# Attention stage: value products of four key pairs in one run, and the denominators of an octet as one round of 512 and one of 256 columns

## The chip, the cores and the metric

The program runs on one core of one Trainium2 chip. The number that counts is the device time of one execution in microseconds. The kernel before took 5224.2 us, the median of three runs (5220.57, 5224.20 and 5231.23).

## What is computed

Two layers follow one another on an image of 512 channels and 64 x 64 pixels (4096 tokens), in float32. The change is in the first one's attention: 16 heads of 32 channels, each a full softmax over 4096 x 4096 scores.

```python
q_in = x
qn = group_norm(x, gn_w, gn_b)
vn = group_norm(qn, gn_w, gn_b)
q, k, v = to_tokens(conv1x1(qn, wq, bq)), to_tokens(conv1x1(vn, wk, bk)), to_tokens(conv1x1(vn, wv, bv))
attn = jax.nn.softmax(jnp.einsum('bhnd,bhmd->bhnm', q, k) * scale, axis=-1)
out = jnp.einsum('bhnm,bhmd->bhnd', attn, v)
out = conv1x1(out.transpose(0, 1, 3, 2).reshape(B, C, H, W), wo, bo)
return (out + q_in) / jnp.sqrt(jnp.float32(2.0))
```

The second layer (a projection, a 5x5 depthwise convolution, linear attention, a projection with batch norm) is not touched.

## The kernel before

The program has five stages in a row, with all engines meeting between them: `stage_qkv`, `stage_attention`, `stage_output`, `stage_linear`, `stage_project`. Only `stage_attention` changes, and it is the longest one.

**Units, pairs, octets.** The stage works through 64 units, 4 per head, of 1024 queries each. A unit goes over 32 key tiles of 128 keys. Two key tiles are a pair (16 per unit), and four pairs are an octet (4 per unit). Eight units (two heads) are a turn; the first and the last turn are written out, and the six between them are a hardware loop.

**The products of TensorE.** For each key tile there are two score products (L642) into one of three PSUM banks `pscore`, 512 queries each. In between go the maximum products (L629): the scores of a unit that is one or two ahead, whose row maxima are needed before its exponentials can be shifted. There are four of them per pair, as many as there are score products, so the two kinds alternate. They go into a ring of four PSUM banks `pmax`. Both kinds are float32r with a stationary operand of 128 columns.

**Value products** (`times_v`, L655) multiply the exponentials of a pair with the values. A pair takes four matmuls of 512 columns (two key tiles by two halves of the queries); each has a stationary operand of 32 columns and writes its own 32 partitions of the bank `pout`, so the four stand side by side in the array. They are plain float32, which TensorE's records show as two instructions each: 8 matmul records for a pair, which are two passes of four side by side. They are issued in runs of `RUN` pairs, at the end of every `RUN`-th pair's scores, for pairs that lie `RUN` to 2 x `RUN` - 1 pairs back.

**Denominators** (`denominators`, L660 to L671) are column sums over the keys. GpSimd adds exponentials beforehand (`eight_steps`, L598 to L611): of the eight tiles in an octet it adds tiles 0, 1, 2 into one sum and 3, 4, 5 into another, and tiles 6 and 7 stay as they are (`RAW` = 6). TensorE then multiplies with a column of ones: four matmuls on the two sums, four on the two raw tiles, 512 columns each, again two records each, so four passes of four. They come once per octet, behind the run of value products of every fourth pair, and go into a bank of the `pmax` ring, which ScalarE copies out (`read_den`, L747).

**What the other engines do.** ScalarE turns each score bank into exponentials (L781), two per key tile, into `prob`, which holds 16 tiles. It also copies `pout` out once per unit (`read_out`, L741) at key tile `OUT_AT` = 2 x `RUN`, the denominators once per octet, and the next head's values once per head (`copy_v`, L756) at key tile 12 of the head's second unit. VectorE takes the row maxima of each `pmax` bank (L808). Once per unit, at pair 14, it reduces them further (`top`, L814); TensorE turns the result (`transpose_shift`, L636) in a bank of the same ring, ScalarE and VectorE split the turned numbers into a high and a low part (L753, L820), and SyncE sends them into the query operand of the next unit. So in that one place a maximum product has only three others between itself and the one whose bank it takes over.

**The order is written out.** Each engine's instructions are issued in program order. A maximum product waits until VectorE has read the bank it takes over, four places back in the ring (`bank_free`). A score product waits for the exponential of the score three back. In `turn` (L685) the order within a pair is: score, maximum, score, maximum, score, maximum, score, then a run of value products and the denominators if they are due, then the fourth maximum.

Of the kernel before, what the change touches and what calls it, by code (L numbers as in the profile page):

```python
# [11 lines left out]
ALU = mybir.AluOpType  # L12
# [8 lines left out]
BANK = 512  # L21
# [5 lines left out]
HD = C // HEADS  # L27
# [7 lines left out]
def done(n):  # L35
    return n + CREDIT
# [306 lines left out]
def stage_attention(nc, x, scr, v_tok, x1, x_in, ident_d):  # L343
# [11 lines left out]
    HS = 2 * KT  # L355
    OCT = 8
    OCTS = KT // OCT
    ADDS = 4
    RAW = 6
    SUMS = 3 * HD  # L360
    FULL = SUMS + 2
    QT = UNIT // P
# [12 lines left out]
    AHEAD = MAXES + EARLY * PER_PAIR  # L375
    T_AT = PER_PAIR

    RUN = 2
    OUT_AT = 2 * RUN
    with ExitStack() as ctx:  # L380
        def sb(name, shape, dt=F32):
            return ctx.enter_context(nc.sbuf_tensor(name, shape, dt))

        def pb(name, shape):
            return ctx.enter_context(nc.psum_tensor(name, shape, F32))

        def sem(name):
            return ctx.enter_context(nc.semaphore(name))
# [4 lines left out]
        prob = sb("b_prob", [P, PBUF, UNIT])  # L393
        sums = sb("b_sums", [P, 2, 2, UNIT])
        ones = sb("b_ones", [P, 1])
# [8 lines left out]
        pmax = [pb(f"b_pmax{i}", [P, BANK]) for i in range(RING)]  # L404
# [8 lines left out]
        exped = sem("b_exped")  # L413
        times_v_done = sem("b_times_v_done")
        pool_added = sem("b_pool_added")
# [180 lines left out]
        @block.gpsimd  # L596
        def _(pool):
            def eight_steps(g, b):  # L598

                p = prob[:, b * OCT:(b + 1) * OCT, :]  # L600


                pool.wait_ge(den_done, done(g - 1))
                for s in range(2):
                    at = 3 * s
                    pool.wait_ge(exped, done((g * OCT + at + 2) * 2))
                    pool.tensor_tensor(sums[:, b, s, :], p[:, at, :], p[:, at + 1, :], ALU.add).then_inc(pool_added, 1)  # L607
                    pool.wait_ge(pool_added, done(g * ADDS + 2 * s + 1))
                    pool.wait_ge(exped, done((g * OCT + at + 3) * 2))
                    pool.tensor_tensor(sums[:, b, s, :], sums[:, b, s, :], p[:, at + 2, :],  # L610
                                       ALU.add).then_inc(pool_added, 1)  # L611

            with pool.Fori(0, ALL * OCTS // 2) as j:
                for b in range(2):
                    eight_steps(j * 2 + b, b)
# [7 lines left out]
        def _(pe):  # L623
# [21 lines left out]
            def times_v(u, head, par, c, pair):  # L645
                if pair == 0:
                    pe.wait_ge(out_read, done(u))
                    if c == 0:
                        pe.wait_ge(v_in, done(head + 1))
                pe.wait_ge(exped, done(u * HS + (2 * pair + 2) * 2))  # L650
                for half in range(2):
                    for odd in range(2):
                        kt = 2 * pair + odd
                        row = (half * 2 + odd) * HD
                        mm = pe.matmul(pout[row:row + HD, :], vst[:, par, kt, :],  # L655
                                       prob[:, kt % PBUF, half * BANK:(half + 1) * BANK],
                                       start=(pair == 0), stop=(pair == PAIRS - 1))
                mm.then_inc(times_v_done, 1)

            def denominators(bank, u, o):  # L660
                pe.wait_ge(pool_added, done((u * OCTS + o + 1) * ADDS))
                pe.wait_ge(exped, done((u * OCTS + o + 1) * OCT * 2))
                for raw in range(2):
                    for half in range(2):
                        for s in range(2):
                            row = (half * 2 + s) * HD
                            terms = prob[:, o % 2 * OCT + RAW + s, :] if raw else sums[:, o % 2, s, :]
                            mm = pe.matmul(pmax[bank][row:row + 1, :], ones[:],  # L668
                                           terms[:, half * BANK:(half + 1) * BANK],
                                           start=(raw == 0), stop=(raw == 1))  # L670
                mm.then_inc(den_done, 1)  # L671

            pe.wait_ge(q_in[0], done(48))
# [11 lines left out]
            def turn(i, first, final):  # L685
                for u, head, par, c in units(i):
# [3 lines left out]
                    for pair in range(PAIRS):  # L690
# [11 lines left out]
                        def one_maximum(n):  # L702
                            if products:
                                bank_free(pe, u, "max", PER_PAIR * pair + n)
                                max_product(bank_of(c, "max", PER_PAIR * pair + n), products[n], t_par, t_buf)

                        for part in range(4):
                            scores(u, 4 * pair + part, par, place % QBUF)
                            if part < 3:
                                one_maximum(part)  # L710
                        if pair % RUN == RUN - 1:
                            for old in range(pair - 2 * RUN + 1, pair - RUN + 1):
                                if old >= 0:
# [3 lines left out]
                        if pair % (OCT // 2) == OCT // 2 - 1:  # L717
                            o = pair // (OCT // 2)
                            if o or behind:
                                bank_free(pe, u, "den", o)  # L720
                                denominators(bank_of(c, "den", o), u if o else u - 1, (o - 1) % OCTS)
# [8 lines left out]
            turn(TURNS - 1, False, True)  # L730
            for pair in range(PAIRS - RUN, PAIRS):
                times_v(ALL - 1, HEADS - 1, 1, UNITS - 1, pair)
            bank_free(pe, ALL, "den", 0)
            denominators(bank_of(0, "den", 0), ALL - 1, OCTS - 1)

        @block.scalar
        def _(act):
# [21 lines left out]
            def unit(u, head, par, c, behind, values, shift):  # L759
                for kt in range(KT):  # L760
# [3 lines left out]
                    if kt % OCT == 0:  # L764

                        act.wait_ge(pool_added, done((u * OCTS + kt // OCT - 1) * ADDS))

# [885 lines left out]
def conv_seq(nc, x, chan, wqT, wkT, wvT, bv, bo, woT, w_all, dw_all, pw_all, wprojT, chan_bn,  # L1653
             group_mean, mask, hmask, ident, out):
    scr = Scratch(nc)
    with nc.sbuf_tensor("v_tok", [P, N // P, C], F32) as v_tok, nc.semaphore("x_in") as x_in:

        x1 = v_tok[:].rearrange("p (k a) c -> p k (a c)", k=KC)
        stage_qkv(nc, x, chan, wqT, wkT, wvT, bv, group_mean, scr, v_tok)
        stage_attention(nc, x, scr, v_tok, x1, x_in, ident)  # L1660
        stage_output(nc, x1, x_in, bo, woT, ident, scr)
        stage_linear(nc, w_all, dw_all, pw_all, mask, hmask, ident, scr, x1)
        stage_project(nc, wprojT, chan_bn, scr, x1, out)
# [49 lines left out]
```

## Time and profile before

| | |
|---|---|
| three runs, median | 5224.2 us |
| the profiled execution | 5231.3 us |
| its span in the trace | 5229.4 us |
| TensorE matmuls busy over the span | 4989.3 us (95%) |
| VectorE busy | 3575.3 us (68%) |
| ScalarE busy | 2878.2 us (55%) |
| GpSimd busy | 2477.0 us (47%) |
| attention stage, from its first maximum product to its last product | 335.6 to about 3858 us |

Busy times are sums over the whole program. Matmul records overlap, so their durations add up to more than the time that passes; the distance between the starts of two neighbours is what one costs. The middle of the attention stage repeats with a fixed period per octet, so one octet read closely stands for some 250.

### The profile page before, as it was taken

The numbers are of one execution on the slowest core, as the hardware profiler recorded it, in microseconds if no ns is written. First come the engines' busy times: TensorE is split into PE (matmuls) and PEld (weight loads), VectorE is DVE, ScalarE is ACT, GpSimd is POOL, SyncE is SP. The second block draws the span as 40 slices with busy tenths as digits, with TensorE's granted clock in tenths as the row PEclk, the third lists the DMA queues.
The fourth block names the chain that finished last, engine by engine and source line by source line (L and its number), as shares of the span: only waits on it lengthen the run. The fifth ranks groups of instructions, "written<-read, shape, count | busy, mean of one in ns | idle before, by whom it ended". The sixth has DMA issues, their size and how long they took to land. (4 is left out here: it accounts for less than half of the span.)

```text
span 5229.4 us, 103029 instructions
## 1 busy us (share of the span) xinstructions
PE 4989.3 (95%) x34768; PEld 2766.3 (53%) x34768; DVE 3575.3 (68%) x4898; ACT 2878.2 (55%) x5445; POOL 2477.0 (47%) x1068
## 2 busy tenths in 40 slices
PE   7989999999999999999999999999978999999697
PEld 6855555555555555555555555555536655555343
DVE  4357777776777777777777777777725887889523
ACT  2216666666666666666666666666651445544402
POOL 0007676776766667667677676677630000000000
PEclk9979999999999999999999999999989999999898
DMA  4330000000000000000000000001031000000254
GB/s 155 129 101 12 24 17 24 24 17 25 17 24 16 26 24 17 25 24 17 25 17 24 25 17 24 17 24 65 22 110 55 12 32 23 31 26 22 80 156 139
DMA packets 101917, 217.38 MB, mean 42 GB/s; under 512 B 13616, under 2 KB 22960, under 8 KB 98864
## 3 DMA queue, kind: packets, MB, share of 16 engines
q1 hardware_dynamic: 101424, 210.81, 12.9%
q8 instruction: 309, 5.06, 0.4%
q14 instruction: 184, 1.51, 0.1%
HBM read 130.54 MB, written 79.69 MB: 40 GB/s over the span
## 5 line engine op out<-in xcount | busy, mean ns | idle before, releaser
L808 DVE TENSOR_REDUCE b_mx<-b_pmax 128x1 f32<-128x512 f32 x4096 | 2507.3, 683 | 935.7 <-PE b_pmax L629 932.9
L781 ACT ACTIVATE b_prob<-b_pscore 128x512 f32<-128x512 f32 x4096 | 2089.8, 619 | 350.1 <-PE b_pscore L642 345.0
L607 POOL TENSOR_TENSOR b_sums<-b_prob 128x1024 f32<-128x1024 f32 x512 | 1220.7, 2384 | 1332.5 <-ACT b_prob L781 1332.5
L629 PE MATMUL b_pmax<-b_kst,b_qst 96*128 96x512 f32 x4096 | 1716.0, 422 | 17.9 <-DMA b_qst<-scratch_ql 15.2
L642 PE MATMUL b_pscore<-b_qst,b_kst 98*128 98x512 f32 x4096 | 1633.7, 400 | 13.8 <-issue 5.0
L610 POOL TENSOR_TENSOR b_sums<-b_sums,b_prob 128x1024 f32<-128x1024 f32 x512 | 1220.5, 2384 | 89.7 <-POOL b_sums L607 86.7
L629 PEld LDWEIGHTS b_pmax<-b_kst,b_qst 96*128 96x128 f32 x4096 | 784.8, 192 | 672.3 <-DVE b_mx L808 287.9
L655 PE MATMUL b_pout<-b_prob,b_vst 128*32 128x512 f32 x8192 | 992.1, 602 | 0.0
L642 PEld LDWEIGHTS b_pscore<-b_qst,b_kst 98*128 98x128 f32 x4096 | 781.0, 191 | 194.2 <-ACT b_prob L781 29.3
L1486 DVE SCALAR_TENSOR_TENSOR d_dsum<-d_ypad,d_dw,d_dsum 128x2048 f32<-128x2048 f32 x288 | 680.9, 2364 | 10.2
L747 ACT ACTIVATE b_outd<-b_pmax 128x512 f32<-128x512 f32 x256 | 153.2, 599 | 765.6 <-PE b_pmax L668 765.6
L655 PEld LDWEIGHTS b_pout<-b_prob,b_vst 128*32 128x32 f32 x8192 | 214.6, 109 | 485.3 <-ACT b_prob L781 282.6
L1397 ACT ACTIVATE d_piece_x<-d_pdw 32x512 f32<-32x512 f32 x384 | 226.3, 589 | 327.0 <-PE d_pdw L1295 313.9
L1250 POOL TENSOR_TENSOR d_num_w<-d_vks,d_mask 128x128 f32<-128x128 f32 x8 | 8.7, 1084 | 799.4 <-ACT d_vks L1438 799.4
L1279 PE MATMUL d_pmain<-v_tok,d_w 128*128 128x512 f32 x768 | 350.7, 600 | 17.7 <-DVE d_tv_x L1462 11.0
L1295 PE MATMUL d_pdw<-d_ypad,d_wtap 32*32 32x512 f32 x9600 | 319.1, 610 | 26.7 <-ACT d_piece_x L1397 25.8
L1295 PEld LDWEIGHTS d_pdw<-d_ypad,d_wtap 32*32 32x32 f32 x9600 | 222.1, 103 | 118.0 <-issue 45.9
L668 PE MATMUL b_pmax<-b_sums,b_ones 128*1 128x512 f32 x2048 | 266.6, 592 | 0.0
L668 PE MATMUL b_pmax<-b_prob,b_ones 128*1 128x512 f32 x2048 | 266.5, 592 | 0.0
L1577 PE MATMUL f_ps<-f_num,f_w 128*128 128x512 f32 x512 | 222.0, 597 | 34.4 <-DVE f_num L1616 34.4
L1279 PEld LDWEIGHTS d_pmain<-v_tok,d_w 128*128 128x128 f32 x768 | 140.7, 191 | 182.1 <-issue 172.3
L1577 PEld LDWEIGHTS f_ps<-f_num,f_w 128*128 128x128 f32 x512 | 98.0, 192 | 159.3 <-issue 159.3
(159 smaller groups left out, 2251.8 us busy)
## 6 DMA issues: line engine op xcount, KB each, us to landing
b_kst<-scratch_kh SPq DMA_DIRECT2D x32, 512.0 KB, 10.5
b_qst<-scratch_qh SPq DMA_DIRECT2D x128, 128.0 KB, 2.9
scratch_att<-b_outn SPq DMA_DIRECT2D x128, 128.0 KB
scratch_num<-d_num SPq DMA_DIRECT2D x64, 256.0 KB, 2.0
f_num<-scratch_num SPq DMA_DIRECT2D x8, 2048.0 KB, 9.7
f_rden<-scratch_rden SPq DMA_DIRECT2D x64, 256.0 KB, 9.7
v_tok<-in_x SPq DMA_DIRECT2D x8, 1024.0 KB, 12.8
scratch_qh<-a_high SPq DMA_DIRECT2D x8, 1024.0 KB, 4.2
```

Of the source, the lines that this page charges most:

```text
L607: pool.tensor_tensor(sums[:, b, s, :], p[:, at, :], p[:, at + 1, :], ALU.add).then_inc(pool_added, 1)
L610: pool.tensor_tensor(sums[:, b, s, :], sums[:, b, s, :], p[:, at + 2, :], ALU.add).then_inc(pool_added, 1)
L629: pe.matmul(pmax[bank][:], qst[0:SUMS, b, t * P:(t + 1) * P], kst[0:SUMS, par, j * BANK:(j + 1) * BANK], start=True, stop=True).then_inc(m ...
L642: pe.matmul(pscore[score_bank(hs)][:], kst[0:FULL, par, kt * P:(kt + 1) * P], qst[0:FULL, b, at], start=True, stop=True).then_inc(scored, 1)
L655: mm = pe.matmul(pout[row:row + HD, :], vst[:, par, kt, :], prob[:, kt % PBUF, half * BANK:(half + 1) * BANK], start=(pair == 0), stop=(pa ...
L668: mm = pe.matmul(pmax[bank][row:row + 1, :], ones[:], terms[:, half * BANK:(half + 1) * BANK], start=(raw == 0), stop=(raw == 1))
L781: act.activation(prob[:, kt % PBUF, half * BANK:(half + 1) * BANK], pscore[score_bank(hs)][:], ACT.Exp, scale=SCALE).then_inc(exped, 1)
L808: dve.tensor_reduce(mx[:, b, t, j:j + 1], pmax[bank][:], AX.X, ALU.max).then_inc(max_read, 1)
L1279: mm = pe.matmul(pmain[:], w[:, b, k, :], x1[:, k, n * BANK:(n + 1) * BANK], start=(k == 0), stop=(k == KC - 1))
L1295: mm = pe.matmul(pdw[r][c * BLK:(c + 1) * BLK, :].rearrange("p (r c) -> p r c", c=IMG), wtap[rows, b, tap, :], ypad[rows, b, y:y + ROWS, d ...
L1486: add = dve.scalar_tensor_tensor(acc, src, dw[:, b, tap:tap + 1], acc, ALU.mult, ALU.add)
L1577: mm = pe.matmul(ps[b * KC + t][:], w[:, m, t * P:(t + 1) * P], num[:, b, m, :], start=(m == 0), stop=(m == MS - 1))
```

## The change

`RUN` goes from 2 to 4: the value products of four pairs stand in one run, at every fourth pair, in front of that octet's denominators. `OUT_AT`, which hangs on it, goes from key tile 4 to key tile 8. `RAW` goes from 6 to 7: GpSimd adds tiles 0 to 3 into one sum and 4 to 6 into the other, five additions instead of four. The one raw tile left is split in columns: of each half of 512 queries, the first 256 columns are added to the rows of the first sum and the other 256 to the rows of the second. So the second round of denominators has four matmuls of 256 columns.

```diff
-    ADDS = 4
-    RAW = 6
+    ADDS = 5
+
+    RAW = 7
...
-    RUN = 2
+    RUN = 4
     OUT_AT = 2 * RUN
...
                 pool.wait_ge(den_done, done(g - 1))
-                for s in range(2):
-                    at = 3 * s
-                    pool.wait_ge(exped, done((g * OCT + at + 2) * 2))
-                    pool.tensor_tensor(sums[:, b, s, :], p[:, at, :], p[:, at + 1, :], ALU.add).then_inc(pool_added, 1)
-                    pool.wait_ge(pool_added, done(g * ADDS + 2 * s + 1))
-                    pool.wait_ge(exped, done((g * OCT + at + 3) * 2))
-                    pool.tensor_tensor(sums[:, b, s, :], sums[:, b, s, :], p[:, at + 2, :],
-                                       ALU.add).then_inc(pool_added, 1)
+                for s, tiles, before in ((0, (0, 1, 2, 3), 0), (1, (4, 5, 6), 3)):
+                    acc = sums[:, b, s, :]
+                    pool.wait_ge(exped, done((g * OCT + tiles[1] + 1) * 2))
+                    pool.tensor_tensor(acc, p[:, tiles[0], :], p[:, tiles[1], :], ALU.add).then_inc(pool_added, 1)
+                    for n, tile in enumerate(tiles[2:]):
+                        pool.wait_ge(pool_added, done(g * ADDS + before + n + 1))
+                        pool.wait_ge(exped, done((g * OCT + tile + 1) * 2))
+                        pool.tensor_tensor(acc, acc, p[:, tile, :], ALU.add).then_inc(pool_added, 1)
...
-                for raw in range(2):
-                    for half in range(2):
-                        for s in range(2):
-                            row = (half * 2 + s) * HD
-                            terms = prob[:, o % 2 * OCT + RAW + s, :] if raw else sums[:, o % 2, s, :]
-                            mm = pe.matmul(pmax[bank][row:row + 1, :], ones[:],
-                                           terms[:, half * BANK:(half + 1) * BANK],
-                                           start=(raw == 0), stop=(raw == 1))
+                for half in range(2):
+                    for s in range(2):
+                        row = (half * 2 + s) * HD
+                        pe.matmul(pmax[bank][row:row + 1, :], ones[:],
+                                  sums[:, o % 2, s, half * BANK:(half + 1) * BANK], start=True, stop=False)
+
+                for half in range(2):
+                    for s in range(2):
+                        row, at = (half * 2 + s) * HD, s * (BANK // 2)
+                        mm = pe.matmul(pmax[bank][row:row + 1, at:at + BANK // 2], ones[:],
+                                       prob[:, o % 2 * OCT + RAW, half * BANK + at:half * BANK + at + BANK // 2],
+                                       start=False, stop=True)
                 mm.then_inc(den_done, 1)
```

TensorE's order at the end of an octet's scores, in the first turn. `b_pmax` are maximum products (and the denominators' bank), `b_pscore` score products, `b_pout` value products. Before:

```order
L629 MATMUL b_pmax3<-b_kst,b_qst 128x512
L642 MATMUL b_pscore1<-b_qst,b_kst 128x512
L629 MATMUL b_pmax0<-b_kst,b_qst 128x512
L642 MATMUL b_pscore2<-b_qst,b_kst 128x512
L655 MATMUL b_pout<-b_prob,b_vst 32x512 x8
L668 MATMUL b_pmax1<-b_sums,b_ones 1x512 x4
L668 MATMUL b_pmax1<-b_prob,b_ones 1x512 x4
L629 MATMUL b_pmax2<-b_kst,b_qst 128x512
```

The same place of the kernel with the change:

```order
L629 MATMUL b_pmax3<-b_kst,b_qst 128x512
L642 MATMUL b_pscore1<-b_qst,b_kst 128x512
L629 MATMUL b_pmax0<-b_kst,b_qst 128x512
L642 MATMUL b_pscore2<-b_qst,b_kst 128x512
L655 MATMUL b_pout<-b_prob,b_vst 32x512 x16
L666 MATMUL b_pmax1<-b_sums,b_ones 1x512 x4
L672 MATMUL b_pmax1<-b_prob,b_ones 1x256 x4
L629 MATMUL b_pmax2<-b_kst,b_qst 128x512
```

Before, eight value products stand here and eight more in the middle of the octet, 8 maximum and 8 score products away on either side. Now all sixteen stand here, and from one such place to the next 16 maximum and 16 score products follow each other with nothing in between.

ScalarE's order around the copy of the value products, before (key tile 4 of a unit). `b_outn` is that copy, `b_outd` the copy of the denominators, `b_prob` the exponentials:

```order
L781 ACTIVATE b_prob<-b_pscore0 128x512 [waits b_scored]
L781 ACTIVATE b_prob<-b_pscore1 128x512 [waits b_scored]
L741 ACTIVATE b_outn<-b_pout 128x512 [waits b_out_stored,b_times_v_done]
L781 ACTIVATE b_prob<-b_pscore2 128x512 [waits b_scored]
L781 ACTIVATE b_prob<-b_pscore0 128x512 [waits b_scored]
```

With the change (key tile 8):

```order
L785 ACTIVATE b_prob<-b_pscore2 128x512 [waits b_scored]
L785 ACTIVATE b_prob<-b_pscore0 128x512 [waits b_scored]
L751 ACTIVATE b_outd<-b_pmax2 128x512 [waits b_den_done,b_den_stored,b_pool_added,b_times_v_done]
L745 ACTIVATE b_outn<-b_pout 128x512 [waits b_out_stored,b_times_v_done]
L785 ACTIVATE b_prob<-b_pscore1 128x512 [waits b_scored]
```

The copy of the value products, which stood alone at key tile 4, now stands right behind that of the denominators at key tile 8.

## Rows read from the trace of the kernel before

**Rows 1.** The page: engines' busy time, TensorE's clock in 40 slices, one group's mean ns.

```profile
PE 4989.3 (95%) x34768; PEld 2766.3 (53%) x34768; DVE 3575.3 (68%) x4898; ACT 2878.2 (55%) x5445; POOL 2477.0 (47%) x1068
...
PEclk9979999999999999999999999999989999999898
...
L668 PE MATMUL b_pmax<-b_sums,b_ones 128*1 128x512 f32 x2048 | 266.6, 592 | 0.0
```

**Rows 2.** Windows, the attention stage's middle: stretch, busy by engine, clock, DMA.

```profile
410.00:3790.00 3380.00, 3368.92 (x19993) 1780.71 (x19995) 2456.70 (x4112) 2222.09 (x4377) 2366.60 (x997) 1.00 0.08 23
```

**Rows 3.** Timeline, TensorE, one octet: start, duration, engine, line, operation.

```profile
1205.82 0.50 PE L629 MATMUL b_pmax<-b_kst,b_qst 96*128 96x512 f32 x1
1206.16 0.39 PE L642 MATMUL b_pscore<-b_qst,b_kst 98*128 98x512 f32 x1
1206.40 0.39 PE L629 MATMUL b_pmax<-b_kst,b_qst 96*128 96x512 f32 x1
...
1209.44 0.39 PE L642 MATMUL b_pscore<-b_qst,b_kst 98*128 98x512 f32 x1
1209.76 1.92 PE L655 MATMUL b_pout<-b_prob,b_vst 128*32 128x512 f32 x16
1211.61 0.50 PE L629 MATMUL b_pmax<-b_kst,b_qst 96*128 96x512 f32 x1
...
1215.55 1.92 PE L655 MATMUL b_pout<-b_prob,b_vst 128*32 128x512 f32 x16
1217.29 1.04 PE L668 MATMUL b_pmax<-b_sums,b_ones 128*1 128x512 f32 x8
1218.15 1.04 PE L668 MATMUL b_pmax<-b_prob,b_ones 128*1 128x512 f32 x8
1219.12 0.50 PE L629 MATMUL b_pmax<-b_kst,b_qst 96*128 96x512 f32 x1
```

**Rows 4.** Timeline, VectorE: the same burst's reads, and the stage's first 64.

```profile
1206.36 4.88 DVE L808 TENSOR_REDUCE b_mx<-b_pmax 128x1 f32<-128x512 f32 x8 [2.63 <-PE b_pmax L629]
...
336.36 38.36 DVE L808 TENSOR_REDUCE b_mx<-b_pmax 128x1 f32<-128x512 f32 x64 [6.25 <-PE b_pmax L629]
```

**Rows 5.** Timeline, the burst with the transposition, three engines.

```profile
1238.21 0.19 PEld L629 LDWEIGHTS b_pmax<-b_kst,b_qst 96*128 96x128 f32 x1 [0.84 <-DVE b_mx L808]
...
1238.75 0.69 DVE L808 TENSOR_REDUCE b_mx<-b_pmax 128x1 f32<-128x512 f32 x1 [0.91 <-PE b_pmax L629]
...
1239.62 3.07 DVE L808 TENSOR_REDUCE b_mx<-b_pmax 128x1 f32<-128x512 f32 x5
...
1240.95 0.19 PEld L629 LDWEIGHTS b_pmax<-b_kst,b_qst 96*128 96x128 f32 x1 [0.23 <-DVE b_mx L808]
...
1241.55 0.19 PEld L629 LDWEIGHTS b_pmax<-b_kst,b_qst 96*128 96x128 f32 x1 [0.30 <-DVE b_mx L808]
...
1242.14 0.19 PEld L629 LDWEIGHTS b_pmax<-b_kst,b_qst 96*128 96x128 f32 x1 [0.30 <-DVE b_mx L808]
...
1242.48 0.39 PE L642 MATMUL b_pscore<-b_qst,b_kst 98*128 98x512 f32 x1
...
1242.80 1.92 PE L655 MATMUL b_pout<-b_prob,b_vst 128*32 128x512 f32 x16
```

**Rows 6.** Timeline, ScalarE, an octet in which the values are copied.

```profile
1098.18 0.60 ACT L747 ACTIVATE b_outd<-b_pmax 128x512 f32<-128x512 f32 x1 [3.23 <-PE b_pmax L668]
1098.67 4.02 ACT L781 ACTIVATE b_prob<-b_pscore 128x512 f32<-128x512 f32 x8
1102.49 1.14 ACT L756 ACTIVATE b_vst<-v_tok 128x1024 f32 x1
1104.34 0.60 ACT L781 ACTIVATE b_prob<-b_pscore 128x512 f32<-128x512 f32 x1 [0.71 <-PE b_pscore L642]
```

**Rows 7.** Timeline, GpSimd, the first two of an octet's four additions.

```profile
1208.74 2.38 POOL L607 TENSOR_TENSOR b_sums<-b_prob 128x1024 f32<-128x1024 f32 x1 [3.44 <-ACT b_prob L781]
1211.29 2.40 POOL L610 TENSOR_TENSOR b_sums<-b_sums,b_prob 128x1024 f32<-128x1024 f32 x1 [0.17 <-POOL b_sums L607]
```

## The prediction, made before the changed kernel ran

> **What bounds the kernel now.** I read the page's engine table first. TensorE is busy 95% of the span, VectorE 68%, and the clock row shows nine tenths or more nearly everywhere [rows 1]. The window over the middle of the attention stage is sharper: of 3380 us TensorE's matmuls fill 3368.9, at a granted clock of 1.00, which is 2.4 GHz [rows 2]. So the stage goes at TensorE's pace, and what matters is what an octet costs there. The timeline gives it to the hundredth: the first maximum product of one octet starts at 1205.82 us and that of the next at 1219.12, so an octet takes 13.30 us [rows 3].
>
> Its parts, all from rows 3. A burst of 8 maximum and 8 score products lasts 3.94 (1205.82 to 1209.76). From the second maximum product at 1206.40 to the last score at 1209.44 there are 13 steps in 3.04, 0.234 each, so a maximum and a score together cost 0.467. A run of value products for two pairs lasts 1.85 in front of a burst (1209.76 to 1211.61) and 1.74 in front of the denominators (1215.55 to 1217.29). The denominators' first two passes take 0.86, so a pass of four matmuls side by side costs 0.43; the last two take 0.97 up to the next maximum product, 0.11 more. The value products' first pass costs 1.74 - 3 x 0.43 = 0.45.
>
> Each change from bursts to runs and back costs 1.85 - 1.74 = 0.11 on leaving a run, 0.34 - 0.23 = 0.11 at the first score after it, 0.32 - 0.23 = 0.09 on entering (1209.44 to 1209.76), and 0.02 in the first pass: 0.33 us. There are two changes per octet.
>
> **Without any wait the change saves 0.76 us per octet.** One of the two changes goes: -0.33. One 512-column round of two passes (0.86) becomes a 256-column round. Nothing in the trace has this shape. Its upper bound is the full pass, 0.43, from the nearest row; the lower one is half of it, 0.215, since a pass's time is that of its columns and the four matmuls of a pass start close together: eight records of 0.592 [rows 1] fill 1.04 us [rows 3], and 1.04 - 0.43 - 0.59 leaves 0.02 for the spread of four starts. I take 0.215, so the round saves 0.43. A price below half would need columns to go faster than they do in any row. Fewer instructions elsewhere are nothing, as they pass beside the array's work.
>
> The Trainium skill has a rule that speaks against half: in "TensorE: Matmul & The Clock Gate" (Part 1) a matmul decoded by the sequencer's own code costs about 62 ns, which bounds small matmuls. Four of them would be an estimated 0.25 us per pass, and the sum would come out 18 us higher; four starts within 0.02 us in the rows speak against it.
>
> **What the long burst adds: VectorE cannot follow it.** VectorE reads 64 banks in 38.36 us, back to back: (38.36 - 0.68) / 63 = 0.598 us from one to the next, with 0.68 for the read itself; the burst's 8 reads give the same (4.88 - 0.68) / 7 = 0.60 [rows 4]. TensorE makes a bank every 0.467 [rows 3]. In a burst of 8 the ring of four banks and the run behind it absorb the difference. In a burst of 16 they don't.
>
> Count from the start of the burst's first maximum product, number 0. VectorE starts reading it 0.54 later (1205.82 to 1206.36), so read k starts at 0.54 + 0.598 k and ends 0.68 later. Maximum product k takes over the bank of k - 4, and its weight load starts about 0.05 after that read's end: in rows 5 the reads that begin at 1239.62 + 0.598 and + 2 x 0.598 end 0.68 later, at 1240.90 and 1241.50, and the loads start at 1240.95 and 1241.55. This gives 0.60 k - 1.12 as the earliest start of load k. Without waiting it starts at 0.35 + 0.467 (k - 1). They cross between k = 7 and k = 8. So before, bursts of 8 (k up to 7) just never waited; with the change every maximum product from the ninth on waits. The last, k = 15, loads at 0.54 + 0.598 x 11 + 0.68 + 0.05 = 7.85. From such a delayed load the score behind it follows 0.34 later and the run 0.32 after that (1242.14, 1242.48, 1242.80, [rows 5]). The burst lasts 7.85 + 0.66 = 8.51, where 16 unhindered ones would take 3.94 + 8 x 0.467 = 7.68. That is 0.83 us of waiting per octet.
>
> The trace of before already contains this wait at full clock, which is why I trust it. In the burst with the transposition the look-back is one shorter, and three maximum loads in a row stand 0.60 apart, each with idle time in front that ends on VectorE's read [rows 5].
>
> The new octet is then 8.51 (burst) + 0.45 + 7 x 0.43 (values, 3.46) + 2 x 0.43 + 2 x 0.215 + 0.11 (denominators, 1.40) = 13.37 us, against 13.30: **+0.07 us**. Over some 250 octets (64 units of 4, less those at the end that have no maximum products) this is +18 us.
>
> **The octet with the transposition.** There VectorE's reduction `top` stands between two reads and pushes the later ones by 0.26: the reads at 1238.75 and 1239.62 are 0.87 apart in place of 0.60 [rows 5]. In the middle of a long burst this delay is no longer absorbed, and the last maximum product looks back three reads, not four: it loads at 0.54 + 0.598 x 12 + 0.26 + 0.68 + 0.05 = 8.71, so the burst lasts 9.37, or 0.86 over the normal one. Before, the same burst lasted 4.59 (1238.21 to 1242.80) against 3.94, 0.65 over. This adds 0.21 in each of 62 units: +13 us. What hangs on the transposition (the split numbers and their transfer into the next unit's queries) has the longer run to hide in, 4.9 us in place of 3.6; nothing there.
>
> **ScalarE.** Exponentials follow each other every (4.02 - 0.60) / 7 = 0.49 us at most [rows 6], slower than scores come unhindered (0.467) but faster than VectorE's 0.598, so ScalarE is the second limit and hidden by the first. The copy of `pout` moves behind that of the denominators and delays the exponentials by 0.5 in one octet of four. Scores then come at 0.49 from the fourth on, 0.25 late, and VectorE's pace has overtaken that by the fifteenth: I take nothing; the bound above is 0.25 in each of 64, 16 us. The value copy (1.14 us) at key tile 12 stood behind a run and was mostly covered by it: it runs from 1102.49 to 1103.63, and the next exponential waits 0.71 for its score [rows 6]. With the change no run stands there. The first exponential comes 1.2 after the burst's start (two copies of 0.5 behind the denominators' end), the ninth 8 x 0.49 and the value copy of 1.0 later, at 6.1; its bank is free at 6.7, and the scores from the twelfth on follow ScalarE at 0.49: the last one at about 8.8 where VectorE alone allows 8.2. That is +0.6 for 15 heads: +9 us.
>
> **GpSimd** gets a fifth addition. It starts its first 2.92 after the octet's start (1208.74) and needs 5 x 2.39 plus three waits on itself of 0.17 [rows 7], 12.46 us, to 15.4. The next octet's first addition comes at 13.37 + 2.92 = 16.3. It keeps up with 0.9 to spare, and the denominators ask for the sums only at the end of the next octet, 9 us later. Nothing.
>
> **Queues.** SyncE's store of `outn` waits for key tile 8 in place of 4, and behind it are the loads of queries three units ahead and of the next head's keys. They are needed more than one unit (53 us) later. Nothing. At the two ends of the stage and at the loop's returns the order shifts by a run; I take nothing, between -5 and +5 us.
>
> **The sum.** 18 + 13 + 9 = +40 us on the profiled execution's 5231.3 (its span of 5229.4 and 1.9 around it), so 5271; that execution is 7.1 over the median of the three runs, so against the median 5224.2 + 40 = **5264 us**. It is a small difference of large terms: -190 us saved (0.76 x 250), +208 us waited (0.83 x 250), and 22 more.
>
> **Rivals.**
>
> *VectorE's pace does not bind.* The place is the wait of maximum products 8 to 15. If bank or read behaved better in a long burst than rows 5 show, TensorE would keep 12.5 us per octet, and GpSimd's 12.46 and ScalarE's 16 x 0.49 would sit just under it: 250 x -0.76 = -190, +9 for the copy, 5043 us. It turns faster from the point at which the wait is under 0.6 us per octet. For it speaks only the average: VectorE is busy 2457 of 3380 us [rows 2]. Against it, the three waiting loads. 0.06.
>
> *The wait is 0.1 us shorter than worked out,* as each term is a reading to a hundredth and the ring starts with some slack. Then all cancels: 5224 to 5234, no difference. 0.10.
>
> *The 256-column round costs more than half.* At the full 0.43 per pass, 2 x 0.215 x 250 = +108: 5372. That it saves nothing gets 0.04; something between (0.25 to 0.3, 5280 to 5305) 0.10.
>
> *ScalarE's two copies in a row are not overtaken.* +16: 5280. 0.06. "TensorEngine Tiling (Array Packing)" in the Trainium skill (Performance Considerations) warns that tiling speeds TensorE and not the emptying of PSUM; that is this rival and my forecast in one, and the rows price it.
>
> The forecast itself has 0.64, with its own range of 5244 to 5285.
>
> **Numbers.** A measurement of this kernel can tell about 0.2%, 10 us, from no change. Below 5214: 0.06. Within: 0.10, mostly the second rival. Above 5234: the rest, 0.84. The range for 8 in 10 goes from 5236 to 5300: it leaves out the two sub-cases on the fast side and the full-price round.
>
> **What the changed profile would show.** Octets of 13.3 to 13.45 us on TensorE's timeline. Reads of VectorE in groups of 16 over 9.65 us (15 x 0.598 + 0.68). Weight loads of the later maximum products 0.60 apart, with idle time that ends on `b_mx`. Idle before them of some 200 us in total that was not there. TensorE's busy share in the middle falls below 99.7%. The last denominators' round 0.43 + 0.11 long. If instead the maximum products stay 0.467 apart to the end of the burst, the forecast is wrong and the kernel is 190 us faster; if the burst is 8.5 and the octet is not 13.4, the 256-column round was mispriced.

## The result, and the profile after

The changed kernel takes 5373.2 us (median of three runs, 5365.4 to 5373.6) against 5224.2 us: a ratio of 1.0278, 95% interval 1.0255 to 1.0302. It is slower, as forecast, but by 149 us where 40 were forecast, and outside the range that ended at 5300. The profiled execution spans 5371.3 us, 141.9 more than before.

First what came as worked out. TensorE's timeline of one octet (start, duration, engine, line, operation), which answers to [rows 3]:

```profile
1236.42 0.50 PE L629 MATMUL b_pmax<-b_kst,b_qst 96*128 96x512 f32 x1
...
1243.08 0.50 PE L629 MATMUL b_pmax<-b_kst,b_qst 96*128 96x512 f32 x1
...
1243.68 0.50 PE L629 MATMUL b_pmax<-b_kst,b_qst 96*128 96x512 f32 x1
...
1244.28 0.50 PE L629 MATMUL b_pmax<-b_kst,b_qst 96*128 96x512 f32 x1
1244.61 0.40 PE L642 MATMUL b_pscore<-b_qst,b_kst 98*128 98x512 f32 x1
1244.94 3.64 PE L655 MATMUL b_pout<-b_prob,b_vst 128*32 128x512 f32 x32
1248.40 1.04 PE L666 MATMUL b_pmax<-b_sums,b_ones 128*1 128x512 f32 x8
1249.26 0.61 PE L672 MATMUL b_pmax<-b_prob,b_ones 128*1 128x256 f32 x8
1249.80 0.50 PE L629 MATMUL b_pmax<-b_kst,b_qst 96*128 96x512 f32 x1
```

The burst takes 8.52 us (1236.42 to 1244.94; forecast 8.51), the value products 3.46 (3.46), the denominators 1.40 (1.40), the octet 13.38 (13.37). The last three maximum products stand 0.60 apart. VectorE's reads and one of the weight loads, answering to [rows 4, 5], show why:

```profile
1236.95 9.66 DVE L812 TENSOR_REDUCE b_mx<-b_pmax 128x1 f32<-128x512 f32 x16 [3.73 <-PE b_pmax L629]
...
1244.28 0.19 PEld L629 LDWEIGHTS b_pmax<-b_kst,b_qst 96*128 96x128 f32 x1 [0.30 <-DVE b_mx L812]
```

Sixteen reads without a gap take 9.66 us, and the load was idle 0.30 us until one of them ended. So a steady octet costs 0.08 us more than before. That cannot make 142 us.

The answer is in the list of who waited for whom (total us, times, longest), in lines for which the trace of before has no counterpart:

```profile
ACT b_outd L751 <- DMA scratch_att_den<-b_outd: 161.0, 18, 9.7
...
PEld b_pmax L629 <- ACT b_outd L751: 75.6, 18, 4.9
PE b_pmax L629 <- ACT b_outd L751: 67.9, 18, 4.5
```

Eighteen times ScalarE's copy of the denominators waited for the store of the previous ones, and TensorE for ScalarE. The timeline of one such place, with ScalarE's instructions and SyncE's transfers (SPq; the duration of such a row spans the issues it groups, and `x4` here is this store's two transfers and, at 1313.06, the next store's two):

```profile
1293.63 0.60 ACT L751 ACTIVATE b_outd<-b_pmax 128x512 f32<-128x512 f32 x1 [4.39 <-PE b_pmax L672]
1294.12 0.59 ACT L745 ACTIVATE b_outn<-b_pout 128x512 f32<-128x512 f32 x1
...
1294.90 1.29 SPq L542 DMA_DIRECT2D scratch_att<-b_outn  x2
1296.48 0.89 SPq L527 DMA_DIRECT2D b_qst<-scratch_qh  x2
1297.47 0.73 SPq L527 DMA_DIRECT2D b_qst<-scratch_ql  x1
1298.40 0.56 SPq L523 DMA_DIRECT2D b_kst<-scratch_kh  x1
1299.05 0.37 SPq L523 DMA_DIRECT2D b_kst<-scratch_kl  x1
1299.52 0.37 SPq L523 DMA_DIRECT2D b_kst<-scratch_kh  x1
1300.14 14.16 SPq L549 DMA_DIRECT2D scratch_att_den<-b_outd  x4
...
1312.27 0.60 ACT L751 ACTIVATE b_outd<-b_pmax 128x512 f32<-128x512 f32 x1 [9.65 <-DMA scratch_att_den<-b_outd]
```

`outd` is one buffer. It is filled at 1293.63; SyncE first stores `outn`, loads queries, and once per head loads the next head's keys (three transfers of 512 KB); the store of `outd` follows at 1300.14. The next copy into `outd` is due at about 1307.3 and starts at 1312.27. The packets of the trace show what the store stood behind: its four rows of 2048 bytes move from 1310.68 to 1311.36, two by two right behind the last two 16 KB packets of the keys, which end at 1310.68 and 1311.03. By the semaphore it has landed at 1312.25, 12.1 us after its issue, and the copy starts.

In the kernel before, `outn` was ready at key tile 4, so the keys were issued half an octet earlier. The store followed its copy by 0.8 us in place of 6.5, and had 12.5 us, not 7, until the next copy (SyncE's and ScalarE's timeline of before):

```profile
1262.20 0.32 SPq L522 DMA_DIRECT2D b_kst<-scratch_kh  x1
...
1264.63 0.60 ACT L747 ACTIVATE b_outd<-b_pmax 128x512 f32<-128x512 f32 x1 [2.94 <-PE b_pmax L668]
...
1265.40 14.56 SPq L548 DMA_DIRECT2D scratch_att_den<-b_outd  x4
...
1277.92 0.60 ACT L747 ACTIVATE b_outd<-b_pmax 128x512 f32<-128x512 f32 x1 [2.93 <-PE b_pmax L668]
```

It stood behind the same keys there and landed at 1275.37, 10.0 us after its issue: 2.5 us before it was needed. So the bytes in front of the store were no harm by themselves; the change took away the room for them.

What it costs TensorE (timeline, then windows with busy time by engine and the granted clock before the last two numbers):

```profile
1308.06 0.39 PE L642 MATMUL b_pscore<-b_qst,b_kst 98*128 98x512 f32 x1
...
1312.92 0.56 PE L629 MATMUL b_pmax<-b_kst,b_qst 96*128 96x512 f32 x1 [4.47 <-ACT b_outd L751]
```

```profile
1308.06:1312.92 4.86, 0.39 (x2) 0.00 (x0) 1.14 (x2) 0.65 (x2) 1.07 (x1) 1.00 0.07 15
1313.00:1320.00 7.00, 7.00 (x17) 5.24 (x18) 5.05 (x8) 5.42 (x10) 4.74 (x3) 0.52 0.01 2
1320.00:1322.40 2.40, 2.40 (x11) 1.73 (x9) 2.40 (x5) 2.19 (x5) 2.40 (x2) 0.99 0.00 0
```

TensorE stands still for 4.5 us, and in the 7 us after it the granted clock is 0.52, the lower level of 1.2 GHz. The burst lasts 15.67 us (1306.78 to 1322.44), 7.1 more than normal. There are 14 such bursts, one per head, 5.8 to 7.3 us too long, 93 us together. In the last turn, where SyncE loads the image at the same place, three more bursts are 3.2, 4.8 and 3.2 too long. That is 104 us of the 142; the first experiment shows that the other 38 are the forecast's own 40.

### The profile page after: what moved, and what is told of

Its sections match the earlier page's. It is cut to its first block and busy times, and to the rows that moved or that the text cites. A ratio compares the mean times of both kernels' runs of the same rounds, so it can differ in the third digit from the quotient of the medians.

```text
span 5371.3 us, 103836 instructions
## 1 busy us (share of the span) xinstructions
PE 5024.1 (94%) x34768; PEld 2708.0 (50%) x34768; DVE 3564.0 (66%) x4898; ACT 2928.4 (55%) x5445; POOL 3079.8 (57%) x1324
## 5 line engine op out<-in xcount | busy, mean ns | idle before, releaser
L785 ACT ACTIVATE b_prob<-b_pscore 128x512 f32<-128x512 f32 x4096 | 2141.6, 637 | 47.7 <-PE b_pscore L642 40.5
L629 PE MATMUL b_pmax<-b_kst,b_qst 96*128 96x512 f32 x4096 | 1831.6, 450 | 87.0 <-ACT b_outd L751 67.9
L611 POOL TENSOR_TENSOR b_sums<-b_sums,b_prob 128x1024 f32<-128x1024 f32 x768 | 1826.6, 2378 | 134.2 <-POOL b_sums L607 85.2
L642 PE MATMUL b_pscore<-b_qst,b_kst 98*128 98x512 f32 x4096 | 1687.8, 414 | 23.4 <-ACT b_prob L785 14.0
L629 PEld LDWEIGHTS b_pmax<-b_kst,b_qst 96*128 96x128 f32 x4096 | 797.4, 195 | 705.5 <-DVE b_mx L812 404.1
L655 PE MATMUL b_pout<-b_prob,b_vst 128*32 128x512 f32 x8192 | 940.4, 600 | 0.0
L642 PEld LDWEIGHTS b_pscore<-b_qst,b_kst 98*128 98x128 f32 x4096 | 796.5, 195 | 265.7 <-ACT b_prob L785 164.5
L655 PEld LDWEIGHTS b_pout<-b_prob,b_vst 128*32 128x32 f32 x8192 | 241.3, 110 | 551.8 <-issue 465.4
L672 PE MATMUL b_pmax<-b_prob,b_ones 128*1 128x256 f32 x2048 | 157.3, 379 | 0.0
## 6 DMA issues: line engine op xcount, KB each, us to landing
b_kst<-scratch_kh SPq DMA_DIRECT2D x32, 512.0 KB, 10.8
```

Source lines behind the costliest of these rows:

```text
L611: pool.tensor_tensor(acc, acc, p[:, tile, :], ALU.add).then_inc(pool_added, 1)
L629: pe.matmul(pmax[bank][:], qst[0:SUMS, b, t * P:(t + 1) * P], kst[0:SUMS, par, j * BANK:(j + 1) * BANK], start=True, stop=True).then_inc(m ...
L642: pe.matmul(pscore[score_bank(hs)][:], kst[0:FULL, par, kt * P:(kt + 1) * P], qst[0:FULL, b, at], start=True, stop=True).then_inc(scored, 1)
L655: mm = pe.matmul(pout[row:row + HD, :], vst[:, par, kt, :], prob[:, kt % PBUF, half * BANK:(half + 1) * BANK], start=(pair == 0), stop=(pa ...
L785: act.activation(prob[:, kt % PBUF, half * BANK:(half + 1) * BANK], pscore[score_bank(hs)][:], ACT.Exp, scale=SCALE).then_inc(exped, 1)
```

## The experiments

Each was timed beside the kernel before on the same chip: 5226.2 us for *the denominators' store first*, *VectorE's pace* and *the two halves*, 5224.5 for *the loads first*, *bytes or moment* and *the version that beats both*.

**The denominators' store first.** The changed kernel, SyncE's part of `turn`:

```diff
                         store_den(*old, OCTS - 2)
                         store(*old)
+                        store_den(*old, OCTS - 1)
...
-                    if not (first and place == 0):
-                        store_den(*old, OCTS - 1)
```

> The changed kernel, with one edit on SyncE: the store of the last octet's denominators is issued right behind the store of the value products, ahead of the loads of queries and keys. Theory A: the 109 us beyond the forecast come from ScalarE waiting for that store, whose transfers stand behind 1.5 MB of keys, once per head. Then the rare bursts of 15 us become normal ones of 8.5 us and the time is 5264 us (5254 to 5275), with octets of 13.38 us as before. Rival B: the long bursts come from something else in the long run (GpSimd's fifth addition, the clock), and the store only happens to be late: the time stays at 5373 us and the idle time moves to another releaser.

Measured: 5268.0 us, ratio 1.0076 (1.0059 to 1.0093). Theory A holds, and B falls: the long run, GpSimd's fifth addition and the rest are all still there. The span is 103.3 us shorter than the changed kernel's, against 104 counted in bursts. SyncE's timeline of it:

```profile
1273.72 1.28 SPq L542 DMA_DIRECT2D scratch_att<-b_outn  x2
1275.26 1.60 SPq L549 DMA_DIRECT2D scratch_att_den<-b_outd  x2
1277.16 1.09 SPq L527 DMA_DIRECT2D b_qst<-scratch_qh  x2
...
1279.12 0.32 SPq L523 DMA_DIRECT2D b_kst<-scratch_kh  x1
```

**The loads first.** The other way out: `store(*old)` moves behind the loads, so that these no longer wait for key tile 8.

```diff
                         store_den(*old, OCTS - 2)
-                        store(*old)
...
                     if not (first and place == 0):
+                        store(*old)
                         store_den(*old, OCTS - 1)
```

> The changed kernel, with the other way out on SyncE: the loads of queries and keys are issued at the unit's start, ahead of the store of the value products, which waits for key tile 8. The keys then have 13 us before the denominators' store is issued behind them. Theory A (that store must not stand behind keys in flight): no burst of 15 us, 5264 us (5258 to 5275), the same as with the store ahead of the loads. Rival: if the number of transfers in the unit's first half as such is the trouble, part of the stalls stays, 5300 us or more.

Measured: 5267.2 us, 1.0087 (1.0070 to 1.0103). Theory A holds. The same transfers, with the same bytes, cost nothing where the store isn't behind keys in flight.

**Bytes or moment.** Key loads of an eighth of the size, in the changed kernel's order:

```diff
-                        load_k(head + 1, 1 - par)
+                        for row, name in ((0, "kh"), (HD, "kl"), (2 * HD, "kh")):
+                            sp.dma_start(kst[row:row + HD, 1 - par, 0:BANK].bitcast(F32),
+                                         heads[name][head + 1, :, 0:BANK]).then_inc(k_in[1 - par], 16)
```

> The changed kernel with SyncE's order as it is, but each of the later heads' key loads brings 512 of the 4096 key positions (the rest keeps older keys, so the attention is that of mixed heads). It tells the bytes in front of the store from the moment at which the store is issued. Theory A1 (the store's transfers stand behind the keys' bytes): it lands in 2 to 3 us and the 15 us bursts are gone: 5264 us. Theory A2 (SyncE issues the store too late, after seven other transfers): the issue stays at 6 us after ScalarE's copy, and part of the stall stays, 5300 us or more.

This kernel leaves out seven eighths of each later head's keys, so its output is not the attention's; only its time is used. Measured: 5276.3 us, one run. Its timeline:

```profile
1272.27 0.60 ACT L753 ACTIVATE b_outd<-b_pmax 128x512 f32<-128x512 f32 x1 [4.39 <-PE b_pmax L674]
...
1278.94 21.37 SPq L549 DMA_DIRECT2D scratch_att_den<-b_outd  x5
...
1285.64 0.60 ACT L753 ACTIVATE b_outd<-b_pmax 128x512 f32<-128x512 f32 x1 [4.38 <-PE b_pmax L674]
```

The store is issued 6.7 us after the copy, as late as in the changed kernel (6.5), and the next copy still comes on time. No burst of 15 us is left. The store has landed at 1284.35, 5.4 us after its issue (A1 had 2 to 3), where it took 12.1 in the changed kernel. So A2 falls, as the late issue alone does not stall anything, and A1 holds in that the keys' bytes fill the time. Together with the kernel before, where the same bytes cost nothing behind an earlier issue, it takes both. From the copy to the landing of its store it is 6.5 + 12.1 = 18.6 us in the changed kernel, more than the 13.4 of an octet; it was 0.8 + 10.0 = 10.8 before, and is 6.7 + 5.4 = 12.1 here. What remains over the 5267 of the kernel with the loads first are the image loads of the last turn, which this kernel does not shorten: its list of waits has `ACT b_outd <- DMA` 4 times, 27 us, and the bursts there are 9 us too long in all.

**VectorE's pace.** The first kernel of this section, with the maxima over half the columns:

```diff
-                dve.tensor_reduce(mx[:, b, t, j:j + 1], pmax[bank][:], AX.X, ALU.max).then_inc(max_read, 1)
+                dve.tensor_reduce(mx[:, b, t, j:j + 1], pmax[bank][:, 0:BANK // 2], AX.X, ALU.max).then_inc(max_read, 1)
```

> The first kernel of this set, with VectorE's maxima taken over 256 of the 512 columns of a bank: the maxima leave out half of the keys, so the shift is another; all else stands. Theory A (VectorE's 0.598 us per read sets the long burst): a read takes some 0.38 us, the waits of maximum products 8 to 15 go, ScalarE's 0.48 to 0.49 us per exponential is the next limit: bursts of 7.7 to 7.9 us, octets of 12.55 to 12.75 us, about 5050 to 5090 us. Rival: if TensorE's own order or ScalarE sets the long burst, it stays at 8.5 us and the time at 5264 us.

Its maxima leave out half of the keys. Measured: 5055.4 us, one run. Sixteen reads now keep up with TensorE, and the burst is 7.73 us long (timeline):

```profile
1240.66 0.50 PE L628 MATMUL b_pmax<-b_kst,b_qst 96*128 96x512 f32 x1
...
1248.39 3.64 PE L654 MATMUL b_pout<-b_prob,b_vst 128*32 128x512 f32 x32
...
1241.20 7.47 DVE L811 TENSOR_REDUCE b_mx<-b_pmax 128x1 f32<-128x256 f32 x16 [5.57 <-PE b_pmax L628]
```

Nothing else was touched, so VectorE's read sets the long burst: 8.52 less 7.73 is 0.79 us per octet, and 5268 less 5055 over some 250 octets is 0.85. At this pace ScalarE's copy of the denominators waits for GpSimd (`ACT b_outd <- POOL b_sums`, 686 us, where the first kernel of this section has 6). GpSimd's 12.46 us are then close to the octet's 12.59 (7.73 + 3.46 + 1.40), so GpSimd is probably the next limit; no run tests that.

**The two halves of the change.** The new denominators with `RUN = 2`:

```diff
-    RUN = 4
+    RUN = 2
```

> The changed kernel with RUN back at 2: only the denominators' part of the change (fifth addition on GpSimd, one round of 512 and one of 256 columns). Theory A: a maximum product never waits in bursts of 8, the round saves 2 x 0.215 us per octet, GpSimd's 12.46 us fit into an octet of 12.87 us, and the key loads are issued at key tile 4 as before the change: 5224 - 0.43 x 256 = 5114 us. Rival C: GpSimd or the ring's last bit of slack takes it back (burst 7 crosses its limit by 0.07 us only): octets of 13.0 to 13.3 us, 5150 to 5224 us.

Measured: 5122.6 us, 0.9800 (0.9783 to 0.9816). Bursts of 8 are 3.94 us as before, the denominators 1.40, the octet 12.87; Theory A holds to 0.2%. GpSimd's five additions of 12.46 us fit in with 0.4 to spare (timeline; the first and the last row are the first additions of two octets, 12.87 us apart, and each waits 0.46 or 0.47 us for ScalarE, and not the other way round):

```profile
1196.27 2.38 POOL L607 TENSOR_TENSOR b_sums<-b_prob 128x1024 f32<-128x1024 f32 x1 [0.47 <-ACT b_prob L785]
...
1206.29 2.39 POOL L611 TENSOR_TENSOR b_sums<-b_sums,b_prob 128x1024 f32<-128x1024 f32 x1 [0.17 <-POOL b_sums L607]
1209.14 2.38 POOL L607 TENSOR_TENSOR b_sums<-b_prob 128x1024 f32<-128x1024 f32 x1 [0.46 <-ACT b_prob L785]
```

And `RUN = 4` with the old denominators, SyncE's store ahead of the loads:

```diff
-    RUN = 2
+    RUN = 4
```

> The kernel before with RUN = 4 only (denominators of two full rounds), and with the denominators' store ahead of the loads so that keys are not in its way. Theory A: per octet -0.33 us for one change of kind less, +0.83 us of waiting for VectorE, so 13.80 us, and 22 us for the transposition and the value copy: 5224 + 125 + 22 = 5371 us. Rival: if the waiting for VectorE is only the shadow of the shorter period, it shrinks where the octet is longer, and the time is 5290 us or less.

Measured: 5379.0 us, 1.0291 (1.0274 to 1.0309). Burst 8.52, values 3.46, denominators 1.83: 13.81 us. Theory A holds, 8 us over its figure, and the rival falls: the burst is as long in an octet of 13.81 us as in one of 13.38, so the wait builds up within the burst.

**A version that beats both.** `RUN = 2`, the new denominators, the loads first:

> A candidate for the fastest: RUN = 2 with the new denominators, and the loads issued at the unit's start. Theory A: in octets of 12.87 us nothing waits for a store (in the run without this edit one burst in 64 is 0.12 us long), so the edit brings nothing: 5114 to 5124 us, the same as without it within 0.2%. Rival: if transfers still delay something that is spread thin, it is 10 us or more faster.

Measured: 5120.2 us, 0.9800 (0.9784 to 0.9816), the same as without the last edit. These two, level within the noise, are the fastest versions here that leave nothing out; what makes them so is the denominators' half of the change.

## Why the prediction was right and wrong, point by point

- *The round of 256 columns costs half.* Right: 0.54 us with the way out (1249.26 to 1249.80), 2 x 0.215 + 0.11, and the records of its two passes start 0.216 apart. The bound that the prediction quoted from the Trainium skill ("TensorE: Matmul & The Clock Gate", Part 1), with the prediction's estimate of 0.25 us per pass, did not show. The half-price round alone is worth 104 us (5122.6 against 5226.2; forecast 110).
- *One change between kinds saves 0.33.* Right: values 3.46 and denominators 1.40 to the hundredth, and with two full rounds 13.81, which is 13.30 + 0.83 of waiting - 0.33.
- *VectorE cannot follow.* Right in mechanism and size: 8.52 for 8.51, and the half reads show it is the cause. One sign was off: the idle time of weight loads that ends on `b_mx` grew by 148 us (287.9 before, 436.2 with the denominators' store first), not by some 200.
- *The transposition's burst.* Forecast 9.37; in the trace 9.38 in most units (1263.20 to 1272.58).
- *The value copy at key tile 12, +0.6.* Right: those bursts last 9.10 us. ScalarE's timeline has the 1.16 us copy at 906.92, and a score product after it waits:

```profile
908.62 0.50 PE L642 MATMUL b_pscore<-b_qst,b_kst 98*128 98x512 f32 x1 [0.69 <-ACT b_prob L785]
```

- *ScalarE's two copies in a row: nothing.* Right. In the octet above, which has both copies, scores are 0.49 apart in the middle, and VectorE's pace has overtaken that at the end.
- *GpSimd: nothing.* Right.
- *Queues: nothing.* This is the step that failed. It followed the moved store to the loads behind it, asked when their data are needed, found a whole unit of room, and stopped. It did not go on to what stands behind the loads: the store of `outd`, a single buffer that ScalarE refills every octet. The loads were not late; they made late what came after them. It cost 103 us (span of 5371.3 against 5268.0 with that store first), where the forecast had nothing; its -5 to +5 was for the stage's ends and the loop's returns.

The sum of all other steps, +40 us, was measured as +42 (5268.0 against 5226.2) and +43 (5267.2 against 5224.5) once that one thing was taken out. The number 5372, which the text gave to a round that saves nothing, lies at the result by chance: the round saved its half.

## What to carry to other kernels

When a change moves a wait on a queue, follow every instruction behind it to the end of the repeating part, and for each ask which buffer it frees, not only which data it brings: a small store from a single buffer behind large loads becomes the critical one. A ring in front of a slower reader covers bursts up to a length that can be counted from the maker's step, the reader's step, the ring's depth and the delays from a product to its read and back; batching work beyond it pays back the saved switch and more. Take a change apart before giving it up: one half of this one was worth 104 us, and the other cost more than that (145 us with the store moved, 5268.0 against 5122.6, and 105 more without).

## What the runs showed of the hardware

Four float32 matmuls of 256 columns, side by side with one output row each, take 0.216 us per pass, half of 512 columns (0.43). A pause of TensorE of 4.5 us was followed by 7 us at a granted clock of 0.52, so a copy that started 5.0 us late made the burst 7.1 us longer. A store behind 1.5 MB of loads on the same queue had landed 12.1 us after its issue in one place of the changed kernel, and 10.0 us after it in one of the kernel before; behind an eighth of the key bytes it had landed after 5.4, and was never waited for at a head's change.
